# A third partial sum for the first 64 expert tiles of a gated-recurrence and mixture-of-experts kernel

## The reference

```python
x = x + layernorm(attn(layernorm(x)))     # gates = x W_in^T W_gate^T + b; a scan over time c = f*c + i*cd; rms norm; h W_out^T
x = x + layernorm(ffn(layernorm(x)))
# ffn: logits = x W_r^T + b_r over 16 experts; the 4 best of each token, softmax over them
# per expert e: g, u = x gate_up[e] + bias;  g = min(g, 7);  u = clip(u, -7, 7)
#   out[e] = ((u + 1) * g * sigmoid(1.702 * g)) down[e] + bias[e]
# result = sum over e of score[token, e] * out[e]
```

## Time and profile before

| | us |
|---|---|
| three runs | 735.36, 728.56, 734.72 |
| median of the runs | 734.72 |
| profiled execution | 727.89 |
| its span, first to last instruction | 726.1 |

### The profile page before, as it was taken

The page is one execution under the profiler, slowest core; times in us unless marked ns, Lnnn a source line. Parts: engine busy times, 40 slices in busy tenths (PEclk is TensorE's granted clock), DMA queues, the critical chain, the costliest instruction groups (busy, mean ns, idle before and its releaser), DMA issues.

```text
span 726.1 us, 13245 instructions
## 1 busy us (share of the span) xinstructions
PE 624.9 (86%) x3666; PEld 403.3 (56%) x3666; DVE 515.6 (71%) x1472; ACT 458.4 (63%) x929; POOL 391.5 (54%) x298
## 2 busy tenths in 40 slices
PE   6987989697989948799989999999999999997640
PEld 2454646363755636466656666666666666664420
DVE  3727587887688887977877767777777777760794
ACT  3688696656486454576756767677676767662044
POOL 0003213246677765677877777665666666675022
PEclk9999898988899965999999999999999999997555
DMA  7978799773232325556778887776776776744998
GB/s 240 417 322 144 235 231 315 178 220 119 99 119 90 123 103 148 146 120 117 127 129 176 177 156 124 117 114 101 118 111 102 121 111 107 116 55 57 337 211 144
DMA packets 110694, 114.32 MB, mean 157 GB/s; under 512 B 31426, under 2 KB 100306, under 8 KB 108962
## 3 DMA queue, kind: packets, MB, share of 16 engines
q0 software_dynamic: 34784, 49.70, 39.5%
q1 hardware_dynamic: 75842, 63.79, 29.4%
HBM read 54.94 MB, written 58.51 MB: 156 GB/s over the span
## 4 chain that ended last, share of the span: by engine, by line
PE 62%; DVE 13%; DMA 9%; ACT 8%; issue 4%; POOL 2%; SPq 0%; DVEq 0%; ACTq 0%; POOLq 0%
PE PS L544 8%; PE PS L696 8%; PE PS L695 8%; PE PS L694 8%; DMA routed<-arena,small 6%; PE PS L708 4%; PE PS L722 4%; PE PS L723 4%; PE PS L683 4%; PE PS L724 4%; PE PS L579 3%; ACT arena L783 2%; PE PS L554 2%; PE PS L601 2%; DMA sums<-arena 2%
## 5 line engine op out<-in xcount | busy, mean ns | idle before, releaser
L1075 POOL DMA_INDIRECT sums<-arena x143 | 223.5, 1563 | 99.6 <-DMA sums<-arena 47.7
L1043 POOL DMA_INDIRECT routed<-arena,small x104 | 114.9, 1105 | 74.2 <-DMA routed<-arena,small 58.7
L544 PE MATMUL PS<-arena 128*128 128x512 f32 x256 | 130.5, 653 | 7.6 <-ACT arena L783 7.4
L1465 DVE TENSOR_SCALAR arena<-PS,small 128x256 f32<-128x256 f32 x143 | 77.7, 544 | 81.4 <-ACT arena L976 80.1
L976 ACT ACTIVATE arena<-PS,small 128x256 f32<-128x256 f32 x143 | 67.9, 475 | 98.8 <-PE PS L696 98.8
L783 ACT ACTIVATE arena<-PS 128x512 f16<-128x512 f16 (+1 forms) x179 | 104.1, 590 | 30.3 <-PE PS L522 9.3
L694 PE MATMUL PS<-W,arena 128*128 x286 | 108.8, 380 | 0.0
L695 PE MATMUL PS<-W,arena 128*128 x286 | 108.7, 380 | 0.0
L696 PE MATMUL PS<-W,arena 128*128 x286 | 108.6, 380 | 0.0
L544 PEld LDWEIGHTS PS<-arena 128*128 128x128 f32 x256 | 50.8, 209 | 63.8 <-issue 59.9
L722 PE MATMUL PS<-W,arena 128*128 x286 | 78.3, 274 | 6.5 <-DVE arena L1439 5.0
(11 more groups left out here) (183 smaller groups left out, 1017.5 us busy)
## 6 DMA issues: line engine op xcount, KB each, us to landing
arena<-routed SPq DMA_DIRECT2D x143, 128.0 KB, 2.5
W<-w_gu SPq DMA_DIRECT2D x8, 1024.0 KB, 24.1
W<-neg_mem POOLq DMA_DIRECT2D x16, 512.0 KB, 11.0
sums<-zero SPq DMA_DIRECT2D x2, 4096.0 KB, 36.1
W<-sums SPq DMA_DIRECT2D x16, 512.0 KB, 8.8
X<-x SPq DMA_DIRECT2D x8, 512.0 KB, 5.8
W<-w_dn SPq DMA_DIRECT2D x4, 1024.0 KB, 11.3
out<-X SPq DMA_DIRECT2D x7, 512.0 KB, 3.2
```

The lines of the kernel that those rows point to most:

```text
L544: last = mm(PS[:, 2 + c % 2, :], WcT[:, k, c * P:(c + 1) * P], xT[:, k, :], start=(k == 0), stop=(k == KT - 1))
L1043: pool.indirect_dma_start(routed, bass.IndirectOffsetOnAxis(ap=idx, axis=0), rows[b][:, jk // TOPK, :], None).then_inc(rows_sent[lane], 16)
L1075: pool.indirect_dma_start(sums[j % SUMS], bass.IndirectOffsetOnAxis(ap=dst[j % MU], axis=0), yb[u], None, compute_op=ALU.add).then_inc(y_s ...
L1465: L.send(v.tensor_scalar(up[j % 2], acc[:, FF:2 * FF], gu_hi, gu_lo, ALU.min, ALU.max))
```

## The change

There is a third sum in memory, `sums_early`, with 2560 rows (blocks 0 to 4). SP zeroes it behind the other two. The first 64 tiles add into `sums[0]`, `sums[1]` and the third in turn, and a scatter waits for the last one before it that went to the same sum. When SP has issued the loads of tile 88 (`THIRD_AT`), it waits for the last 12 early scatters and for what used the SBUF before, and loads the third sum's five blocks into `z3` (four in X's ring, one in W). At the end, SP loads `sums[0]` for all blocks and `sums[1]` for blocks 5 to 7 only; POOL waits for all scatters and adds `sums[1]` of blocks 0 to 4 onto `z3` by accumulating loads. `total` reads `z3` in place of `z2` for these blocks. DVE's, ACT's and PE's instructions stay as many.

```diff
@@ -59,6 +59,8 @@
 MAGIC = float(0x5F1FFFF9)
 ROOT_A, ROOT_B = 0.375 * 0.703952253, 0.375 * 0.703952253 * 2.38924456
 SUMS = 2
+THIRD = EARLY_AT + 1
+THIRD_AT = 88
 BATCHES = ((0, 1, 2, 3), (4, 5, 6), (7,))
 PART = 1024
 PARTS_GU, PARTS_DN = E * KT * 2 * FF // PART, E * KT * DIM // PART
@@ -153,7 +155,7 @@
         routed16 = routed.bitcast(f16)
         pairs = routed.rearrange("r (c two) -> (r c) two", two=2)
         sums = [nc.dram_tensor(f"sums{a}", [TOKENS + (E + SPARE) * P, DIM], f32, kind="Internal").ap() for a in range(SUMS)]
-
+        sums.append(nc.dram_tensor("sums_early", [THIRD * BLK, DIM], f32, kind="Internal").ap())
 
         X = sb("X", [P, XRING * BT, DIM])
 
@@ -227,6 +229,8 @@
         sT = [W[0:E, (SUMS * NBLK * PART + g * BLK):(SUMS * NBLK * PART + (g + 1) * BLK)] for g in range(NBLK)]
         z, z2 = [[W[:, n * PART:(n + 1) * PART].rearrange("p (u d) -> p u d", u=BT) for n in range(a * NBLK, (a + 1) * NBLK)]
                  for a in range(SUMS)]
+        z3 = [X[:, BT * m:BT * (m + 1), :] for m in (3, 4, 0, 1)]
+        z3.append(W[:, (SLOTS - 1) * PART:SLOTS * PART].rearrange("p (u d) -> p u d", u=BT))
 
 
         sat = [0]
@@ -320,6 +324,7 @@
         y2_ready = sem("y2_ready")
         y_sent = [sem(f"y_sent{u}") for u in range(YU)]
         z2_in = [sem(f"z2_in{n}") for n in range(NBLK)]
+        z3_in = [sem(f"z3_in{n}") for n in range(THIRD)]
         zero_ready, zero_sent, x1_sent = sem("zero_ready"), sem("zero_sent"), sem("x1_sent")
         sT_mm, sT_ready = sem("sT_mm"), sem("sT_ready")
         bias_mm, t_ready, rz_ready, yz_ready = sem("bias_mm"), sem("t_ready"), sem("rz_ready"), sem("yz_ready")
@@ -359,6 +364,14 @@
         def acc_bank(j):
 
             return j % 3 if j < HEAD else j % 2 if j < EARLY else (j - EARLY + 2) % 3
+
+        def sum_of(j):
+
+            return j % (SUMS + 1) if j < EARLY else j % SUMS
+
+        def sent(j):
+
+            return y_sent[j % YU], 16 * (j // YU + 1)
 
         def x2T_bank(t, k):
 
@@ -451,6 +464,8 @@
             for a in range(SUMS):
                 sp.dma_start(sums[a][0:TOKENS, :].rearrange("(n p) d -> p n d", p=P),
                              zero[:, :].unsqueeze(1).to_broadcast([P, NTILE, DIM])).then_inc(zero_sent, 16)
+            sp.dma_start(sums[SUMS].rearrange("(n p) d -> p n d", p=P),
+                         zero[:, :].unsqueeze(1).to_broadcast([P, THIRD * BT, DIM])).then_inc(zero_sent, 16)
             ring_x(XRING + 1)
             sp.wait_ge(minus_done, 16 * E)
             sp.wait_ge(bias_out, 16)
@@ -495,13 +510,22 @@
                 sp.dma_start(meta[j % MU], pairs[ds(pairs_at[j], P, ROW // 2), :]).then_inc(meta_in[j % MU], 16)
                 if 0 <= j - PADS_AT < E:
                     pad(j - PADS_AT)
+                if j == THIRD_AT:
+                    for i in range(EARLY - YU, EARLY):
+                        sp.wait_ge(*sent(i))
+                    sp.wait_ge(low_done, PARTS)
+                    sp.wait_ge(x2_ready, NBLK - 1)
+                    sp.wait_ge(x1_sent, 16 * (NBLK - 1))
+                    for g in range(THIRD):
+                        sp.dma_start(z3[g], sums[SUMS][BLK * g:BLK * (g + 1), :].rearrange("(u p) d -> p u d", p=P)).then_inc(z3_in[g], 16)
 
 
             for u in range(YU):
                 sp.wait_ge(y_sent[u], 16 * len(range(u, TILES, YU)))
             for g in range(NBLK):
                 sp.dma_start(z[g], sums[0][BLK * g:BLK * (g + 1), :].rearrange("(u p) d -> p u d", p=P)).then_inc(blk_in[g], 16)
-                sp.dma_start(z2[g], sums[1][BLK * g:BLK * (g + 1), :].rearrange("(u p) d -> p u d", p=P)).then_inc(z2_in[g], 16)
+                if g >= THIRD:
+                    sp.dma_start(z2[g], sums[1][BLK * g:BLK * (g + 1), :].rearrange("(u p) d -> p u d", p=P)).then_inc(z2_in[g], 16)
             g = NBLK - 1
             for h in range(2):
                 sp.wait_ge(last_ready, h + 1)
@@ -1068,15 +1092,22 @@
                 u = j % YU
                 pool.wait_ge(meta_in[j % MU], 16 * (j // MU + 1))
                 if j == 0:
-                    pool.wait_ge(zero_sent, 16 * SUMS)
+                    pool.wait_ge(zero_sent, 16 * (SUMS + 1))
                 pool.wait_ge(y2_ready, j + 3)
-                if j >= SUMS:
-                    pool.wait_ge(y_sent[(j - SUMS) % YU], 16 * ((j - SUMS) // YU + 1))
-                pool.indirect_dma_start(sums[j % SUMS], bass.IndirectOffsetOnAxis(ap=dst[j % MU], axis=0),
+                same = [i for i in range(j) if sum_of(i) == sum_of(j)]
+                if same:
+                    pool.wait_ge(*sent(same[-1]))
+                pool.indirect_dma_start(sums[sum_of(j)], bass.IndirectOffsetOnAxis(ap=dst[j % MU], axis=0),
                                         yb[u], None, compute_op=ALU.add).then_inc(y_sent[u], 16)
                 if j % 2 and j // 2 < 2 * BT * TOPK - AHEAD:
                     late_row(j // 2)
 
+            for j in range(TILES - YU, TILES):
+                pool.wait_ge(*sent(j))
+            for g in range(THIRD):
+                pool.wait_ge(z3_in[g], 16)
+                pool.dma_start(z3[g], sums[1][BLK * g:BLK * (g + 1), :].rearrange("(u p) d -> p u d", p=P),
+                               accum_op=ALU.add).then_inc(z2_in[g], 16)
             pool.wait_ge(x1_sent, 16 * (NBLK - 1))
             for g in range(NBLK - 1):
                 pool.wait_ge(yz_ready, g + 1)
@@ -1477,7 +1508,7 @@
 
 
             def total(g):
-                flat, flat2 = [a[g].rearrange("p u d -> p (u d)") for a in (z, z2)]
+                flat, flat2 = [a.rearrange("p u d -> p (u d)") for a in (z[g], z3[g] if g < THIRD else z2[g])]
                 bias = PS[:, 2 * (g % 3):2 * (g % 3) + 2, :].rearrange("p b x -> p (b x)")
                 dve.wait_ge(blk_in[g], 32)
                 dve.wait_ge(bias_mm, g + 1)
```

## The result

The changed kernel takes 743.58 us in the median of 12 runs (737.08 to 749.60); the kernel before took 735.37 on the same chip (12 runs, 728.56 to 738.80). The ratio is 1.0116, with an interval of 1.0080 to 1.0152. It is 8.2 us slower. The forecast was 738 us, from a sum of +5.6.

What follows compares the result with a forecast made beforehand. PE and DVE bound the attention part, PE the tile loop, DVE is busiest in the end; POOL finishes 10.9 us late. Terms +10 - 6.9 + 0.5 + 2 = +5.6 on the mean 731.6 gave 737, nudged to 738; range 726 to 748.

Steps and rivals of the forecast that it cites:

- POOL's gain: Tile loop: three sums use up POOL's delay of 9.55 us, 2 us stay, last scatter earlier; -6.9 us, low end 4.
- the zeroing: Attention part: third zeroing on SP's queue delays block 6's load from 139.16 to about 149; +10 us, ends 5 and 14.
- the loads: Tile loop: five 512 KB loads of the third sum ahead of row tile 89; +0.5 us, range 0 to 3.
- the tail: End: POOL's first addition lands after 7.5 us, DVE 2.5 us later, then keeps pace; +2 us, range 0 to 6.
- I count the stall in full: Attention part: PE and ACT follow DVE's norms and can't run ahead, so block 6's whole stall counts; 10 us.
- as POOL's pace is PE's, what delay there is stays: Tile loop after tile 64, two sums alternating again: POOL's delay remains about 2 us to the end.
- PE should not wait: Tile loop: SP is 8 row tiles, 19 us, ahead; the 2.6 MB of loads take 7 to 14 us.
- rival 2: Loop and tail: loads at tile 88 throw POOL back and additions run late; +13.5 us, 745; chance 0.16.
- a scatter that gives way to single packets of 1 KB should lose tenths only: Tile loop: argument against scatter pairs stretching by a microsecond each beside the loads at tile 88.
- rival 4: End: the first addition is quick, so the tail costs nothing; +3.6 us, 735; chance 0.06.
- Rival 1: Attention part: zeroing hidden in DVE's wait or stall swallowed; -6.9 to -3.9 us, about 726; chance 0.22.
- Rival 3: Tile loop: third sum does nothing for POOL, since issuing, not landing, keeps it late; +12.5 us, 744; chance 0.08.

Runs made afterwards that it cites:

- e4: Changed kernel with the third zeroing at 31 us, third sum neither loaded nor added, end of the kernel before: 724.71 us, ratio 0.9885 to the kernel before.
- e5: e4 with the five loads of the third sum put back in the tile loop, still not added: 728.25 us, ratio 0.9940 to the kernel before.
- e2: Changed kernel with the third zeroing moved ahead to 31 us, behind the store of the negated rows: 735.70 us, ratio 1.0050 to the kernel before.
- e1: Kernel before with only the third zeroing added, at the change's place, that sum otherwise unused: 739.47 us, ratio 1.0110.
- e8: Kernel before with its two zeroings moved to 31 us: 733.53 us, ratio 1.0011.
- e3: e2 with the third sum loaded in 20 pieces of 128 KB, one every second tile from tile 88: 734.48 us, ratio 1.0048 to the kernel before.
- e12: e9 with PE's first bias earlier, block 4's addition later, third sum loaded at tile 76 instead of 88: 730.37 us, ratio 0.9986 to the kernel before.
- e7: e6 with all three zeroings at 31 us: 750.26 us, ratio 1.0223 to the kernel before.
- e6: e2 with the end's blocks in the order 5, 6, 0, 1, 2, 3, 4, 7: 735.73 us, ratio 1.0030 to the kernel before.
- e9: e2 with SP loading both sums of all blocks and DVE, not POOL, adding the third sum: 732.24 us, ratio 1.0001 to the kernel before.

## Why the prediction was right and wrong

The sign and about the size were right: slower by 5.6 us forecast, 8.2 measured. Of the four terms POOL's gain came out near its size and the zeroing at about half of it or more; the loads and the tail cost far more than forecast. The terms are priced by ratios times 733 us, each known to 3 or 4 us either way, starting from the kernel before:

| step | runs compared | forecast, us | measured, us |
|---|---|---|---|
| third sum for POOL, zeroed early, not read | before, e4 | -6.9 | -8.4 |
| loading it during the tiles | e4, e5 | +0.5 | +4.0 |
| POOL's additions in the end | e5, e2 | +2 | +8.1 |
| third zeroing at its place, not early | e2, after | +10 | +4.8 (8.1 alone, e1) |
| sum | before, after | +5.6 | +8.5 |

The steps are one chain from before to after, so the measured column must add up to the ratio of the change. That the forecast sum is only 2.9 us off is in part luck: loads and tail were 9.6 us too cheap, the zeroing and POOL's gain 6.7 too pessimistic. And the +1 to +11 that the prediction gives its forecast "by its bounds" is narrower than what the bounds of its terms add up to, -1.9 to +19.

*Zeroing.* Place and mechanism were right: packet for packet beside POOL's loads, block 6's statistics at 150.71 where 149 was forecast. The term of 10 came out as 8.1 us alone (e1) and 4.8 when it is moved (e2); which is nearer is open. What did not hold is "I count the stall in full": of 14.0 us more wait in the changed kernel 10.1 arrive at the first output tile, of 7.8 more in e1's trace 3.7, and of the 5 to 7 us in the late traces of the last section nothing that shows.

*POOL caught up.* The 64th scatter starts 0.7 us behind its tile, and three sums alone are worth 8.4 us. The step that failed is "as POOL's pace is PE's, what delay there is stays". With two sums the delay came back by itself: in e4, with no loads, it is 2.9 to 6.8 us from tile 72 to 139 and 7.8 at the last tile, not 2. So SP's first load followed the last tile by 11.6 us in e4 and by 13.4 in the changed kernel, where 6 to 9 was forecast. That e4 is nevertheless 8.4 us faster, when its last scatter is only 3.1 us nearer its tile than in before's trace, may lie in that trace. The traces of e1 and e8, which keep the tile loop of before, have 13.1 and 16.1 us at the last tile (e8: ready at 657.02, scattered at 673.15) where before's has 10.9; against these e4 is 5.3 and 8.3 us nearer. What a median run has is not known.

*Loads in the loop.* "PE should not wait" held: PE is busy 40.00 of 40.00 us from 490 to 530 in the changed kernel too. But the term looked at the wrong engine. The 2.6 MB delay the landing of scatters, and the 5 us lost at tiles 75 to 78 are not won back in the traces of the changed kernel and of e5 (9.6 and 9.8 us at the last tile). That they must stay is not shown: in e2's trace, with the same loads, the delay fell from 8.5 us at tile 94 to 4.4 at tile 139, and ended at 6.5, below the 7.8 of e4 without loads. So the price of 4.0 rests on the runs of e4 and e5. It was rival 2's mechanism, of which "a scatter that gives way to single packets of 1 KB should lose tenths only" fell: two pairs took 8.39 and 8.52 us. Neither smaller pieces (e3) nor an earlier place (e12) mend it.

*The tail.* This step was wrong by the most. "With 0.4 us to issue and the loads of the first sum beside it I take 7.5" became 10.9, and DVE was 6.4 us later instead of 2.5 (11.45 against 5.05 us behind SP's first load). The row used was of accumulating stores that had the DMA engines to themselves; here SP's loads were in the queues beside it, packet for packet. The pace of 4.1 us per block was about right: the waits that followed were 0.44 and 0.90 us. The rule of the Trainium skill weighed in the prediction (page "DMA: Bandwidth & Descriptors", section "Anatomy of one DMA") gives an estimate of 3.2 us for 512 KB; the measured 10.9 decides, and rival 4 falls. The Trainium skill, in the section "Queues, rings and completion order" of the same page, says that a DMA engine takes its queues in turn, by packets; the traces agree, with 477 to 477 and 717 to 716 packets.

Rival 1, that the zeroing is hidden, fell with the 14.72 us wait and the 10.1 us at the first output tile; its second ground, that the attention part swallows a stall, held for a part of it. Rival 3 fell with the 0.7 us at tile 63.

## What to carry to other kernels

A burst of DMAs is not free where the engine that computes has its data: ask which small transfers share the queues with it, and whether the engine that waits for their landing has any reserve to win the time back. Price an accumulating DMA by a row in which other queues are loaded, since it takes turns with them by packets and slows them as well. A zeroing or any other big write is paid by what stands behind it on its issuing queue, so look there for the next load that an engine waits for. Do not take that wait as the price: follow it to the next stage, since a part of it, or all, can be gone there.

## What was not expected of the hardware

The load of block 6 is a race that kernels with the same queue in front of it win or lose. Ten traces have only the two old zeroings ahead of it (all but after, e1, e7 and e8). The store of block 1, whose landing the load waits for, was issued between 106 and 112 us in all ten, and SP's queue needed 8.5 to 11.0 us to issue it. SP's row of that store and POOL's row of its last four accumulating loads, in e3 and then in e4:

```profile
106.82 10.38 SPq L457 DMA_DIRECT2D out<-X  x1
...
117.68 4.92 POOL L1078 DMA_DIRECT2D W<-neg_mem  x4 [21.87 <-ACT W L901]
```

```profile
108.33 11.01 SPq L457 DMA_DIRECT2D out<-X  x1
...
117.03 4.92 POOL L1068 DMA_DIRECT2D W<-neg_mem  x4 [19.70 <-ACT W L891]
```

In e3 POOL comes 0.5 us behind the end of SP's row (117.20), in e4 2.3 us ahead of it (119.34). This splits all ten: in before, e3, e5 and e6 POOL came 0.5 to 2.8 us behind that end, and the load went out at 126.95 to 128.46; in e2, e4 and e9 to e12 it came 1.7 to 2.3 us ahead of it, and the load went out at 137.36 to 139.10, so that DVE waited 5.4 to 7.0 us. That the order decides is inferred from these ten; no run sets it.

As unexpected is that losing the race costs nothing that the traces show. The first output tile was ready between 303.6 and 307.2 us in the six late traces and between 300.9 and 307.6 in the four others. From 155 to 190 us, behind the stall, TensorE's granted clock (1 is full speed) was 0.94 to 0.95 on average in five of the late six (0.85 in e9) and 0.80 to 0.90 in the other four. Whether that is what gives the time back is not shown.
